# First alibi pass inside the last rope sequence, second pass from its end on, and far ranks by ScalarE

## The chip, the cores and the metric

The kernel runs on one core of one Trainium2 chip. The metric is the device time of one execution in microseconds, the median of several runs. All times of the profile come from one profiled execution.

## What is computed

Four layers over a tensor of 4 sequences of 512 tokens with 128 channels. Each layer normalises its input, computes an attention-like branch `s` and a gate `g` from a mixture of experts, and adds their product:

```python
xn = _layernorm(x); s = attn(xn); g = _silu(ffn(xn)); x = x + s * g
```

The change touches the end of layer 2 (rope attention, eight small experts) and layer 3. In layer 2

```python
att_num = exp(q_rope @ k_rope * scale)
att_den = sum(exp(q @ k * scale), axis=-1)
y = (att_num / att_den) @ v
```

In layer 3, 16 heads of width 8 with a linear bias by distance, and an expert layer with 16 experts that each take the 160 tokens which chose them with the highest probability:

```python
scores = q @ k.T / sqrt(8) - abs(i - j) * 0.5**h
out = softmax(scores) @ v
top1_val, top1_idx = probs.max(-1), probs.argmax(-1)
masked = where(top1_idx == expert, top1_val, -inf)
vals, idx = top_k(masked, 160)        # ceil(1.25 * 2048 / 16)
y[idx] = gelu(x[idx] @ W1 + b1) @ W2 + b2   # tokens not taken keep their input
```

## The kernel before

**Lists of steps.** `flow()` returns one list of steps (what, layer, sequence, number). Each engine's program walks the same list and issues its share of each step, so this list, written by hand, is the order of TensorE, VectorE, ScalarE, GpSimd and the DMA queue of SyncE. Engines are coupled by semaphores only. The last rope sequence stands in `rope_alone()`, layer 3 in `last_layer(tail)`, where `tail` is the end of the last rope sequence ("t" 0 to 3: turn the heads, project, combine, norm and turn).

**Scores.** A unit is two banks of PSUM, 1024 columns: two heads by one block of 128 keys or queries. A quad is four heads. For the alibi layer each sequence has 32 first-pass units ("a", `scores_a`, lines 1200 and 1214), each of which VectorE reduces to negated row maxima (`maxima`, line 2088), and 32 second-pass units ("b", `scores_b`, lines 1253, 1273 and 1277), whose exponential ScalarE takes (`probabilities`, line 1674). Between them stands "mx": the maxima are turned on TensorE (line 1222), split in two, and go through DRAM into rows of the second pass's operand (`maxima` of SyncE). A rope sequence has no maxima: 32 plain units (line 1260), whose exponentials are only summed (line 1657), and 32 rotated ones (line 1264, exponential on line 1674). "pv" multiplies probabilities with values (`values`, line 1295, for the alibi layer, `grain_values`, line 1314, for the others), "bc" turns the sums and divides ("heads").

**Two slots.** The four banks of scores are two slots. They are given to "a" and "b" units in turn, in the order of the list, whatever their kind. A unit waits until the unit before the last has been read.

**Buffers.** Rope and causal probabilities go through a ring of four buffers ("grains") of two units each. The alibi layer has two buffers of four units each. Its operands are three stacks for each parity of the sequence, `stacks3`; those of sequence 0 are filled by DMA after the rope list has ended (`part_out`, line 2372: six DMAs for each of queries and keys; `last_stacks`, line 2376: 24 DMAs; `rows`), the rest after that.

**Order of layer 3.** The rope list ends; then 32 "a" units of sequence 0 stand alone with the rope tail, the expert logits ("lg", line 1116), their softmax ("sm", `route_softmax` and `route_parts`), eight transposes ("tn") and 12 ranks. Then for b = 1, 2, 3: second pass of sequence b - 1 with the 32 "a" units of sequence b spread among it. Sequence 3's second pass comes last.

**Ranks.** 64 steps "rk" (`route_row`, line 1131, and `route_rank`, line 2010). Step n compares 128 tokens (block n // 4) with 512 tokens (sequence n % 4): TensorE writes a row of 512 values, VectorE counts in one pass how many are above the token's own. The 16 steps in which the 512 hold the 128 (near ranks) are cut in two pieces and have a third operation for ties. After 16 ranks "sl" makes slot numbers, with which GpSimd scatters tokens to DRAM. After the last it loads all slots (line 2282); "xt" turns them, "eu" and "ed" are the experts in pairs (gelu on line 1722), "xb" turns them back (line 1728), and GpSimd writes them (line 2284) and gathers them by token (line 2289, 16 gathers), after which "t" 2 of each sequence ends the layer.

## Time and profile before

| | us |
|---|---|
| median of 3 runs (lowest to highest) | 1894.1 (1892.93 to 1896.52) |
| time of the profiled execution | 1889.69 |
| its span, first to last instruction | 1887.6 |
| PE busy | 1542.4 (82%) |
| DVE busy | 1178.3 (62%) |
| ACT busy | 995.9 (53%) |
| POOL busy | 206.5 (11%) |
| mean granted TensorE clock | 0.866 of 2.4 GHz |

PE is TensorE's matmuls, DVE is VectorE, ACT is ScalarE, POOL is GpSimd, SPq SyncE's DMA issues. Matmuls are pipelined, so busy PE time is longer at the lower of TensorE's two clock levels (1.2 GHz, a granted clock of 0.5) and says nothing of how well the array is filled. Times in the trace are microseconds from the start of the span. In a row of a stretch, busy times are sums in us inside it, (x) is the count of instructions, PEclk the mean granted clock. In a row of the timeline, the first number is the start, the second the length; brackets name idle time of that engine just before and what ended it.

### The profile page before, as it was taken

Reading aid. Unit: us, or ns where it says so; the run is one execution under the profiler, and the core shown is the slowest. Engines: PE = TensorE matmul, PEld = TensorE weight load, DVE = VectorE, ACT = ScalarE, POOL = GpSimd, SP = SyncE. Lnnn points to the kernel's source line nnn. Section 1 sums busy time; section 2 is a strip of 40 time slices with the busy share of each in tenths; the row PEclk is TensorE's granted clock in tenths of the full one; section 3 lists DMA queues with packets and bytes.
Section 4 is the critical chain, followed back from the end, with each engine's and each line's share of the span. In section 5 each row is a group of like instructions: output and inputs, shape, how many; then the busy total and the mean of one; then the engine's idle time right before and its main releaser. Section 6 shows DMA issues by size and latency. Waiting matters only on the chain. (4 is left out here: it accounts for less than half of the span.)

```text
span 1887.6 us, 23967 instructions
## 1 busy us (share of the span) xinstructions
PE 1542.4 (82%) x8656; PEld 778.0 (41%) x8656; DVE 1178.3 (62%) x2370; ACT 995.9 (53%) x1642; POOL 206.5 (11%) x152
## 2 busy tenths in 40 slices
PE   5999989988699588977889778897586578878886
PEld 2555556555355244433444334443232322323442
DVE  4789989999765853456534665335425787776522
ACT  4787778866123147633666326654574122333675
POOL 1333342432000000000000000000000000001003
PEclk9999999999899799978998789986666567888999
DMA  4422232353301120203002030001402142122002
GB/s 169 119 75 73 78 81 68 90 143 93 106 19 51 51 60 10 63 22 101 19 1 76 9 101 19 18 1 36 109 19 83 46 164 59 33 65 60 1 2 73
DMA packets 91621, 116.30 MB, mean 62 GB/s; under 512 B 10096, under 2 KB 71536, under 8 KB 91120
## 3 DMA queue, kind: packets, MB, share of 16 engines
q1 hardware_dynamic: 89808, 110.05, 20.8%
q0 software_dynamic: 1696, 4.72, 0.9%
q8 instruction: 69, 1.13, 0.3%
q14 instruction: 48, 0.39, 0.1%
HBM read 83.27 MB, written 31.46 MB: 61 GB/s over the span
## 5 line engine op out<-in xcount | busy, mean ns | idle before, releaser
L1674 ACT ACTIVATE scratch<-ps 128x1024 f32<-128x1024 f32 x272 | 271.3, 1022 | 218.8 <-PE ps L1270 69.7
L2088 DVE TENSOR_REDUCE neg_max<-ps 128x2 f32<-128x1024 f32 (+2 forms) x224 | 234.4, 1068 | 97.8 <-PE ps L1214 97.0
L1657 ACT ACTIVATE ps<-ps 128x512 f32<-128x512 f32 x256 | 150.0, 586 | 84.4 <-PE ps L1260 83.9
L1945 DVE TENSOR_TENSOR_SCAN scratch<-scratch 128x512 f32<-128x512 f32 x128 | 159.5, 1286 | 3.5 <-ACT scratch L1628 3.4
L1853 DVE SCALAR_TENSOR_TENSOR gated<-tanh,ps 128x512 f32<-128x512 f32 x88 | 60.4, 687 | 135.9 <-ACT tanh L1556 135.8
L1314 PE MATMUL ps<-scratch,values 128*32 128x512 f32 (+3 forms) x1024 | 129.7, 598 | 10.4 <-ACT scratch L1674 9.0
L1556 ACT ACTIVATE tanh<-ps 128x512 f32<-128x512 f32 x88 | 52.3, 595 | 160.0 <-PE ps L995 159.7
L1030 PE MATMUL ps<-xnt,weights_even 128*128 128x512 f32 x256 | 125.5, 612 | 7.5 <-ACT gated L1539 6.6
L2268 POOL TENSOR_SCALAR variance_eps<-mean_var 128x4 f32<-128x4 f32 x20 | 5.3, 264 | 978.2 <-DVE mean_var L1773 978.2
L995 PE MATMUL ps<-xnt,weights_odd 128*128 128x512 f32 x176 | 109.6, 708 | 0.0
L2101 DVE COPY head_out<-ps 128x512 f32<-128x512 f32 x48 | 33.0, 688 | 117.0 <-PE ps L1314 76.5
L998 PE MATMUL ps<-xnt,weights_odd 128*128 128x512 f32 x176 | 97.9, 639 | 7.0 <-DVE values L2070 7.0
L1674 ACT ACTIVATE weights_even<-ps 128x1024 f32<-128x1024 f32 x64 | 64.8, 1024 | 72.3 <-PE ps L1277 71.7
L1214 PE MATMUL ps<-scratch 52*128 52x256 bf16 (+7 forms) x704 | 96.3, 343 | 0.0
L1017 PE MATMUL ps<-weights_odd,hidden 128*128 128x128 f32 x640 | 94.5, 292 | 0.0
L1017 PEld LDWEIGHTS ps<-weights_odd,hidden 128*128 128x128 f32 x640 | 81.1, 197 | 29.9 <-issue 28.0
L2307 POOL TENSOR_TENSOR weights_odd<-weights_odd,scratch 128x512 f32<-128x512 f32 x32 | 72.4, 2262 | 170.7 <-DVE scratch L1952 170.3
L1260 PE MATMUL ps<-scratch 48*128 48x512 bf16 x256 | 61.1, 441 | 33.9 <-ACT ps L1657 25.3
L1200 PE MATMUL ps<-consts,scratch 128*128 128x128 bf16 x256 | 42.2, 255 | 55.6 <-DVE neg_max L2088 51.6
L2307 POOL TENSOR_TENSOR scratch<-scratch 128x512 f32<-128x512 f32 x32 | 67.8, 2118 | 131.9 <-DVE scratch L1952 131.7
L1067 PE MATMUL ps<-scratch,consts 128*128 128x512 f32 x128 | 71.4, 641 | 12.5 <-DVE scratch L1952 12.3
L1264 PE MATMUL ps<-scratch 48*128 48x512 bf16 x256 | 57.4, 454 | 29.5 <-DVE neg_max L2088 12.1
(324 smaller groups left out, 2917.6 us busy)
## 6 DMA issues: line engine op xcount, KB each, us to landing
scratch<-state_rows SPq DMA_DIRECT2D x64, 512.0 KB, 4.9
scratch<-parts_scratch SPq DMA_DIRECT2D x288, 96.0 KB, 2.4
parts_scratch<-weights_even SPq DMA_DIRECT2D x168, 128.0 KB, 2.4
weights_odd<-in_l SPq DMA_DIRECT2D x8, 519.5 KB, 6.4
weights_even<-in_l SPq DMA_DIRECT2D x1, 4096.0 KB, 15.9
weights_odd<-in_l SPq DMA_DIRECT2D x1, 4096.0 KB, 12.9
parts_scratch<-gated SPq DMA_DIRECT2D x15, 128.0 KB, 2.4
slots_scratch<-head_out SPq DMA_DIRECT2D x5, 256.0 KB, 5.2
```

Of the source, the lines that this page charges most:

```text
L995: pe.matmul(ps[:, UP, :], W(l, "w1")[:, P * f:P * (f + 1)], tokens(b), start=True, stop=True)\
L998: pe.matmul(ps[:, MI, :], W(l, "w3")[:, P * f:P * (f + 1)], tokens(b), start=True, stop=True)\
L1017: mm = pe.matmul(ps[:, YB, P * j:P * (j + 1)], buf[lo:lo + n, P * j:P * (j + 1)], W(l, "w2")[lo:lo + n, P * src:P * (src + 1)], start=(one ...
L1030: pe.matmul(ps[:, up_bank(0, n), :], W(0, "w1")[:, P * f:P * (f + 1)], tokens(n // NF[0]), start=True, stop=True).then_inc(q[0, "up_ready" ...
L1067: pe.matmul(ps[:, 0, :], eye, hc[n % 3][:, 0, :], start=False, stop=True, skip_group_check=True)\
L1214: mm = pe.matmul(place(col + c0, c1 - c0), lhs, stack_of(l, b, 1 + turn)[p0:p0 + KA[l], s, c0:c1], start=False, stop=True, skip_group_chec ...
L1314: mm = pe.matmul(ps[32 * i:32 * i + 32, PV, q0:q0 + n], vx[l - 1][:, c, VW * h:VW * h + 32], grain(l, b, s)[:, place_, col:col + n], start ...
L1657: ins = act.activation(bank, bank, ACT.Exp, accum_out=dens[:, j, h:h + 1])
L1674: act.activation(dst, src, ACT.Exp).then_inc(q[l, "exp_done"], 1)
L1945: dve.tensor_tensor_scan(hs[:, g, :], da[n % RING][:, g, :], ub[:, g, :], 0.0, ALU.mult, ALU.add)\
L2088: ins = dve.tensor_reduce(dst, ps[:, base:base + 2, col:col + n], AX.X, ALU.max, negate=True)
L2307: pool.tensor_tensor(y1[b % 2], y1[b % 2], hc[n % 3][:, 1, :], ALU.add)\
```

## The change

- The alibi units of the first pass are listed before those of the second, and values go one key block at a time: 16 stages of two units for each sequence in place of 8 of four in two parts. The product is `grain_values` for all layers; `values` goes.
- The ring becomes seven places. Layer 3 uses places 2 and 4 for its first sequence and 2, 4, 5, 6 for the others; the last rope sequence uses three in place of four.
- `stacks3` of sequence 0 moves to space that is free while rope runs; that of sequence 1 takes the space of rope's stacks and two grains.
- `rope_alone` lists the 32 first-pass units of alibi sequence 0 among quads 1 to 3 of the last rope sequence, with the queries and keys of alibi sequences 0 and 1, "mx" of sequence 0 before the last units, and the DMA steps for it.
- `last_layer` begins with the second pass of sequence 0: its first 20 items stand without first-pass units, beside the tail, logits and softmax; the 32 first-pass units of sequence 1 follow. Ranks: 16, 30 and 18 beside b = 1, 2, 3, in place of 12 before b = 1 and 26, 26 and 0. Four expert pairs stand in b = 3 and four in the last pass, in place of five and three.
- Far ranks (48 of 64) go to ScalarE: a Sign with the token's scaled value as bias into SBUF, then a Relu with an accumulator. Near ranks stay on VectorE. Each kind has its own semaphore, and the slot step has two more small VectorE operations.

The core of the diff:

```diff
             sums = [[(h, j, 512 * k, 512) for k, h in enumerate(hp)] for j in range(TB) for hp in pairs]
-            for cp in range(2):
-                for n in range(4):
-                    unit = sums[4 * cp + n]
-                    units_a.append(unit)
-                    units_b.append((len(stages), n, unit))
-                stages.append((g, cp, len(units_b), 2))
+            units_a += sums
+            for j in range(TB):
+                for n in range(2):
+                    units_b.append((len(stages), n, sums[2 * j + n]))
+                stages.append((g, [(j, 0, 0, 512)], len(units_b)))
...
-    out = with_extras(a[0], extras) + [("mx", l, 0, 0)] + ranks(6, 12)
-    cuts = [12, 38, RANKS]
+    out, cuts = [], [0, 16, 46, RANKS]
     for b in range(1, NB):
         main = stream[begin[b - 1]:begin[b]]
-        cover = len(main) - 10
-        main = spread(main[:cover], a[b]) + [("mx", l, b, 0)] + main[cover:]
-        extras = [(18, ("v", l, b, 0))] if b > 1 else [(2, ("v", l, 1, 0))]
+        cover, alone = len(main) - 10, 20 if b == 1 else 0
+        main = main[:alone] + spread(main[alone:cover], a[b]) + [("mx", l, b, 0)] + main[cover:]
+        route = ranks(cuts[b - 1], cuts[b])
+        if b == 1:
+            out.append(tail[0])
+            extras = [(1, tail[1]), (5, tail[2]), (8, ("v", l, 1, 0)), (12, tail[3])]
+            extras += [(14, ("lg", l, 0, 0)), (15, ("sm", l, 0, 0)), (18, ("sm", l, 0, 1))]
+            extras += [(22 + 2 * k, ("tn", l, 0, k)) for k in range(8)]
+            extras += [(40 + 40 * n // len(route), item) for n, item in enumerate(route)]
+        else:
+            extras = [(18, ("v", l, b, 0))]
         if b + 1 < NB:
-            extras += [(34, ("q", l, b + 1, 0)), (40, ("q", l, b + 1, 1))]
...
+            extras += [(44, ("q", l, b + 1, 0)), (50, ("q", l, b + 1, 1))]
+        if b == 2:
             extras += [(3 + 78 * n // len(route), item) for n, item in enumerate(route)]
-        else:
-            extras += [(28 + 3 * n, ("xt", l, 0, n)) for n in range(ST // 4)]
-            for p in range(5):
-                extras += [(44 + 8 * p, ("eu", l, 0, p)), (48 + 8 * p, ("ed", l, 0, p))]
+        if b == 3:
+            extras += [(n, item) for n, item in enumerate(route)]
+            extras += [(40 + 3 * n, ("xt", l, 0, n)) for n in range(ST // 4)]
+            for p in range(4):
+                extras += [(54 + 8 * p, ("eu", l, 0, p)), (58 + 8 * p, ("ed", l, 0, p))]
...
-    extras += [(18 + n, ("xb", l, 0, n)) for n in range(ST // 4)]
+    for p in range(4, PAIRS):
+        extras += [(2 + 5 * (p - 4), ("eu", l, 0, p)), (4 + 5 * (p - 4), ("ed", l, 0, p))]
+    extras += [(23 + n, ("xb", l, 0, n)) for n in range(ST // 4)]
...
+    a = [("a", 3, 0, n) for n in range(2 * TB * QUADS)]
+    groups = [(rope_sums(c, g),) + rope_group(c, g) for g in range(QUADS)]
+    sums, group, bc = groups[0]
+    out += weave(sums, tail2[0:2] + head[5:7])
+    out += weave(group, tail2[2:3] + [("mb0", 2, c, 0), ("mb1", 2, c, 0), ("set", 3, 0, 0), ("q", 3, 0, 0)]) + [("q", 3, 0, 1)]
+    sums, group, last = groups[1]
+    out += [("ld", 2, c, 2)] + later(weave(later(sums, bc), tail2[3:4] + d[0:2]), u[0:2], 4)
+    out += weave(group, a[0:4], d[2:4]) + u[2:4]
+    sums, group, bc = groups[2]
+    out += [("ld", 2, c, 3)] + weave(later(sums, last), a[4:11], d[4:6])
+    out += weave(group, a[11:18], d[6:8])
+    sums, group, last = groups[3]
+    out += weave(later(sums, bc), a[18:25], [("v", 3, 0, 0), ("q", 3, 1, 0)])
+    out += weave(group[:6], a[25:32], [("q", 3, 1, 1)]) + [("mx", 3, 0, 0), ("ld", 3, 1, 0)] + group[6:]
+    return out + [last], [("t", 2, c, k) for k in range(4)]
...
-        pt3 = [scratch[:, 12288:16384].rearrange("p (i c) -> p i c", i=4), wa[:, PT_AT:PT_AT + 4096].rearrange("p (i c) -> p i c", i=4)]
+        ring = [v.rearrange("p (i c) -> p i c", i=4) for v in
+                [scratch[:, n:n + 2048] for n in (8192, 10240, 12288, 14336, 4096)] + [wa[:, n:n + 2048] for n in (PT_AT, PT_AT + 2048)]]
+                    for n in ns] for ns in ((0, 1, 7), (3, 4, 5))]
...
+            if l == 3:
+                return (2, 4, 5, 6) if b else (2, 4)
+            return (0, 1, 2) if l == 2 and b == NB - 1 else (0, 1, 2, 3)
...
+                def rank_far(n):
+
+                    i, c = n // TB, n % TB
+                    above = c > i // TB
+                    act.wait_ge(q[3, "row_ready"], n + 1)
+                    done, count = ranked(n)
+                    if count > 2:
+                        act.wait_ge(done, count - 2)
+                    sign = r_sign[count % 2]
+                    own.link(act.activation(sign, ps[:, route_bank(n), :], ACT.Sign, scale=-RANK_SCALE, bias=r_v[:, 1, i:i + 1]))
+                    counter = c if above else 6 + c
+                    act.activation(sign, sign, ACT.Relu, scale=-1.0 if above else 1.0,
+                                   accum_out=r_acc[:, i, counter:counter + 1]).then_inc(done, 1)
...
+                elif what == "q" and l == 3 and b == 1:
+                    part_out(l, b, n)
+                elif what == "ld" and l == 3:
+                    sp.wait_ge(q[2, "pv_done"], NS[2] * NB)
+                    rows(l, odd=True)
+                    last_stacks(b)
+                    load_columns(3, at["l3"]["w1"][0], wide["l3"], s_w[3])
...
+                elif what == "mx" and (l == 1 or b == 0):
+                    maxima(l, b)
+                elif what == "q" and l == 3 and b == 0:
+                    part_out(l, b, n)
                     if n == 1:
-                        rows(3)
...
+                        sp.wait_ge(q[fourth[0], "pv_done"], fourth[1])
+                        rows(l)
+                        last_stacks(b)
```

## Rows read from the trace of the kernel before

**Rows 1.** Busy time by stretch; columns as in the first line, us.

```profile
core 0: us, PE busy (x) PEld busy (x) DVE busy (x) ACT busy (x) POOL busy (x), PEclk, DMA share, GB/s
1330.00:1391.00 61.00, 45.67 (x208) 20.25 (x208) 19.04 (x76) 43.00 (x91) 2.53 (x4) 0.61 0.25 67
1391.00:1442.00 51.00, 38.83 (x188) 13.47 (x185) 13.11 (x37) 37.53 (x84) 0.00 (x0) 0.70 0.28 80
1442.00:1530.50 88.50, 55.63 (x278) 26.78 (x276) 71.99 (x173) 8.25 (x14) 2.53 (x4) 0.54 0.22 62
1530.50:1627.80 97.30, 79.72 (x519) 26.34 (x518) 71.50 (x146) 32.91 (x33) 7.95 (x8) 0.77 0.25 84
1627.80:1724.10 96.30, 78.07 (x552) 26.62 (x550) 71.88 (x151) 34.52 (x35) 6.66 (x7) 0.84 0.16 46
1724.10:1815.90 91.80, 77.33 (x622) 37.24 (x620) 49.72 (x61) 54.56 (x68) 2.36 (x3) 0.93 0.09 24
1815.90:1872.00 56.10, 49.24 (x419) 22.47 (x418) 8.65 (x20) 46.66 (x57) 12.76 (x13) 1.00 0.14 37
1872.00:1887.60 15.60, 2.41 (x16) 1.74 (x16) 9.32 (x15) 2.78 (x5) 3.77 (x4) 0.73 0.32 88
```

**Rows 2.** Waits of TensorE, 1442 to 1530.5: us in total, times, longest.

```profile
PE ps L1200 <- DVE neg_max L2088: 23.4, 12, 8.6
```

**Rows 3.** Timeline of TensorE: logits, turning of maxima, first unit of the second pass.

```profile
1472.73 7.01 PE L1116 MATMUL ps<-weights_odd,xnt 128*128 128x16 f32 x32
...
1523.28 1.01 PE L1222 MATMUL ps<-consts,neg_max 128*16 128x128 f32 x4 [0.62 <-DVE neg_max L2088]
...
1530.56 0.42 PE L1253 MATMUL ps<-consts,scratch 128*128 128x128 bf16 x2
```

**Rows 4.** Timeline of TensorE: a rope unit, values, a first-pass unit (two rows).

```profile
1402.93 0.61 PE L1264 MATMUL ps<-scratch 48*128 48x512 bf16 x2 [1.04 <-ACT ps L1657]
...
1406.49 1.93 PE L1314 MATMUL ps<-scratch,values 128*32 128x512 f32 x8
...
1448.92 0.39 PE L1200 MATMUL ps<-consts,scratch 128*128 128x128 bf16 x2
1449.24 0.61 PE L1214 MATMUL ps<-scratch 52*128 52x512 bf16 x2
```

**Rows 5.** Groups of VectorE instructions, 1627.8 to 1724.1: busy us, mean ns | idle before.

```profile
L2088 DVE TENSOR_REDUCE neg_max<-ps 128x2 f32<-128x1024 f32 x32 | 39.1, 1223 | 14.4 <-PE ps L1214 14.3
L2010 DVE TENSOR_SCALAR_CACHE_REDUCE weights_even<-ps,weights_even 128x512 bf16<-128x512 f32 (+3 forms) x32 | 20.2, 644 | 4.2 <-PE ps L1131 4.0
...
L2010 DVE DVE_READ_ACCUMULATOR weights_even<-ps,weights_even 128x1 f32 x32 | 2.6, 83 | 0.0
```

**Rows 6.** Groups of ScalarE instructions, 1391 to 1442.

```profile
L1657 ACT ACTIVATE ps<-ps 128x512 f32<-128x512 f32 x32 | 18.6, 583 | 3.1 <-PE ps L1260 3.1
L1674 ACT ACTIVATE scratch<-ps 128x1024 f32<-128x1024 f32 x16 | 15.5, 1020 | 6.9 <-PE ps L1264 6.9
L1657 ACT ACTIVATION_READ_ACCUMULATOR ps<-ps 128x1 f32 x32 | 6.0, 187 | 0.0
...
L1641 ACT ACTIVATE queries_keys<-ps,small_l 128x512 f32<-128x512 f32 x1 | 0.7, 688 | 1.1 <-PE ps L1165 1.1
```

**Rows 7.** Timeline of TensorE: turning of the normed rows of rope sequence 2.

```profile
1352.54 1.09 PE L982 MATMUL ps<-consts,branch 128*128 128x128 f32 x4 [5.00 <-DVE branch L1786]
```

**Rows 8.** Timeline of SyncE's DMA queue: stack loads of alibi sequence 0.

```profile
1429.07 11.04 SPq L2376 DMA_DIRECT2D scratch<-parts_scratch  x22
```

**Rows 9.** Groups of ScalarE instructions, 1724.1 to 1872: table loads and gelus.

```profile
L1722 ACT ACT_TABLE_LOAD x8 | 10.3, 1283 | 0.1
...
L1722 ACT ACTIVATE hidden<-ps,weights_odd 128x160 f32<-128x160 f32 x32 | 10.0, 395 | 6.3 <-PE ps L1142 6.2
```

**Rows 10.** Timeline of GpSimd: write of the slots, last of 16 gathers.

```profile
1846.30 1.33 POOL L2284 DMA_DIRECT2D slots_scratch<-weights_even  x1 [117.63 <-ACT weights_even L1728]
...
1877.28 0.94 POOL L2289 DMA_INDIRECT weights_even<-slots_scratch,logits  x1 [0.30 <-issue]
```

169 lines of the change are left out of this document (58 added, 111 removed).

## Prediction

> **What bounds the kernel now.** I read the page for its shares first, then the table of busy time by stretch, cut at the places where the step list changes its work [rows 1], then the waits of TensorE in the stretch that the change empties, then single instructions for prices. Columns of [rows 1] to compare: the length, PE, DVE and ACT busy, and PEclk.
>
> Call the stretches R1 (1330 to 1391) and R2 (1391 to 1442), the last rope sequence; A (1442 to 1530.5), the first alibi pass alone; B0, B1, B2 (to 1627.8, 1724.1, 1815.9), a second pass beside the next first pass; B3 (to 1872), the last second pass; and the tail. In R2 ScalarE works 37.5 of 51.0 us and VectorE 13.1. In A it is the other way round: VectorE 72.0 of 88.5, ScalarE 8.3, TensorE 55.6 at a granted clock of 0.54, so nearly all of it at 1.2 GHz. There TensorE waits 23.4 us for maxima [rows 2]. In B0 and B1 VectorE (71.5 and 71.9) and TensorE (79.7 and 78.1) hold each other up: two score slots are handed out in turn, so a first-pass unit waits for the reduction before it, and that queues behind ranks. In B3 TensorE has 49.2 of 56.1 and ScalarE 46.7. VectorE's surplus in A is thus what the whole end pays for, and the change spreads it.
>
> **The change part by part.** Terms are in the span of the profiled execution, 1887.6 us; its own time is 1889.7, and the median of the three runs 1894.1, 4.4 above it.
>
> *A goes.* Its 88.5 us end [rows 1] with the way of the maxima through DRAM: turned at 1523.28, first second-pass unit at 1530.56, 7.3 us [rows 3]. The new list turns them before the last three rope units; a rope unit with its share of values takes 1.6 us or more (51.0 / 32 in R2), and with three values blocks and the last quad's heads these cover about 8 us. Cover gone, at most 7.3. Term: -88.5.
>
> *R1 and R2 take 32 first-pass units.* Such a unit is 0.39 + 0.61 us of TensorE at the low level [rows 4] (about two thirds of that at 2.4 GHz, an estimate from the L1200 and L1214 lines of other stretches) and one reduction of 1.22 us [rows 5], on a VectorE that has 13.1 us to do in R2. But the slots: rope units now go two to a slot pair with a maxima unit between nearly all of them, so neither kind is double buffered any more. One period of a pair is scores 0.8, reduction 1.22, two handovers of 0.1 to 0.2: 2.3 us, longer than the rope side, which is 0.6 of scores and 2 x 0.583 + 0.19 of exponentials [rows 4, 6]. 28 pairs lie in R2: 64 us. On top come 8 values blocks of 1.93 at the low level [rows 4], taken at 1.4 because part of them fits into the pair's gaps: 11. Projections of queries, keys and values, heads and expert downs: 9. So R2 goes from 51 to 84: +33. In R1, 4 units at 1.2: +5. R1 also gains and loses a wait of the same size: the turning of the normed rows, for which TensorE stood 5.0 us [rows 7], moves later, while the first maxima unit now waits for operands. That DMA queue I followed: six pieces each of queries and keys, 3.8 us each, seven row loads, then 24 stack loads of 0.5 us (22 took 11.04 [rows 8]) with the next rope stack queued behind them. The rope stack has over 20 us to spare; the first quad's stack lands about 5 us after TensorE could use it, and all later rope units would queue behind that unit on TensorE, and ScalarE behind them. I set the two against each other. Term: +38, bounds +22 (pairs at 2.0, values half hidden) and +60 (pairs at 3.0, as in B1, 96.3 / 32).
>
> *B0 changes its inside.* First part: 14 second-pass units without maxima units, at 1.5 us each (B3 gives (56.1 - 3 expert pairs of about 3.8) / 32 = 1.4): 21. Beside them the tail of the rope layer, turns and values (5 us of TensorE), the logits, 7.0 us of TensorE [rows 3], and a softmax behind which ScalarE's exponentials queue because its exp is in the same stream: about 5. Together 38. Its operands (30 loads and the expert weights, released by the last rope values) have these 38 us to land. Second part: 32 maxima units beside 12 second-pass units. VectorE: 32 x 1.22 = 39, parts of the next queries and keys 4.5, heads 3, near ranks 4: 51. TensorE at 2.4 GHz also comes to about 50. Two engines both full and coupled by the slots: 60. The last ten items as now: 9.5. B0 becomes 108: +11, bounds 0 and +22. Only two buffers hold probabilities for this sequence, two units each; the values block that frees one stands ahead of the unit that needs it in TensorE's order, so I price that at 0; so too the two small sums (0.17 each) that each of the four blocks of slot numbers gains.
>
> *Ranks change engine.* A rank costs VectorE 0.64 + 0.08 [rows 5]. 48 of the 64 are far ones. On ScalarE each is two activations: the nearest rows are 0.688 for one with a pointer bias out of PSUM, 0.583 for one with an accumulator and 0.19 for its read [rows 6], and the second waits for the first, so 1.5 us (1.2 if they overlap, 1.8 if each link costs a handover). In B1, 22 of 30 ranks are far: VectorE loses 16 us, ScalarE goes from 34.5 to about 68 of 96.3. Before B1's TensorE was idle for 18.2 us; I take half of that back: -9 (0 to -18). The Trainium skill, ScalarE: Activation LUTs, "Rules for kernel authors", speaks against this edit: it puts max, relu and the like on VectorE, up to three times faster per element. The trace agrees in the ratio (1.5 against 0.72 here); it disagrees in what it is worth, since the row of B1 shows ScalarE idle for two thirds of the time. By the rule alone the edit would cost 48 x 0.8 = 37 us; that is not the sum's value, but near the slower rival below.
>
> In B2, 18 ranks now stand one behind each of the first 18 items. 14 far ones are 21 us of ScalarE beside 8 exponentials, 29 us where these items took 18/85 of 91.8 = 19: +10, less one expert pair, which leaves for B3 (two table loads of 1.283 and four gelus of 0.395 [rows 9], 4.1): +5, bounds -4 and +12. The slots' way through DRAM (17.5 us by the same trace) begins some 25 us later and is asked for 12 items later; 23 items lie between, enough.
>
> *B3 and the tail.* One pair more, 4 us, and the turning back of the slots moves from item 18 to 23: GpSimd's chain of write and gathers, which runs from 1846.3 to the last issue at 1877.3 plus landing [rows 10] and cannot be shortened, starts about 7 us later after B3's begin. It ended just before the last sums now, so most of this shows: +6, bounds +3 and +9.
>
> Sum: -88.5 + 38 + 11 - 9 + 5 + 6 = -37.5. Span 1850.1, profiled time 1852.2, median 1856.6.
>
> **The rivals.**
> *Clock.* With pairs in R2 TensorE is asked for more, and it may be granted 2.4 GHz where it had 0.61 and 0.70 [rows 1]. B2, at 0.93, and B3, at 1.00, where TensorE waits least, show the level held. Then pairs take 2.0, values 1.07, B0 and B1 give 8 each more: about 22 us better, 1834.
> *Slot pairs at the pace of B1.* If coupling costs as much as in B1, 3.0 a pair, R2 gains another 20 and B0 8: 1884. For it: VectorE's stream has expert sums and parts between the reductions. Against: B1's pace holds a rank in each pair.
> *Far ranks on the path (slower).* Place: ScalarE's stream in B0 to B2, where exponentials queue behind a rank and TensorE behind these through the slots. Price: 48 x 1.5 = 72 us if all of it shows, in place of B1's -9. The other terms sum to -28.5, so it decides from 0.6 us a rank. Against: ScalarE is idle 60 us of B1; for: in B2 they come one to every item. With two thirds exposed: -28.5 + 48 = +20, 1914.
> *Table loads (slower).* If Sign were in another table set than the exponential, each far rank would bring two loads of 1.283 [rows 9]: 48 x 2.57 = 123 us of ScalarE, of which at most 60 hides: 1920 or more. No operation of the trace is a Sign. The Trainium skill, same page, "Table sets: the hidden batching unit", says cheap functions stand in every set and names relu but not sign; it prices a switch at 2.66 us, by which this would be 255 us, and which no row here shows (1.283 and 0.1 idle).
> *The move does nothing.* Maxima units in R2 wait for their stacks until rope has ended: then A's reductions come back, +25, 1882. The queue count above speaks against it.
>
> **How the numbers follow.** Forecast (within 15 us of 1856.6) 0.60; clock 0.15; slot pace or late stacks 0.13; far ranks 0.09; table loads 0.03. The range goes from 1830, the clock's case with a margin, to 1888, which holds the slot rival, and leaves out the two slower ones and the extremes. Within 0.2% (3.8 us, about what a measurement of this kernel can tell from no change) lie the mildest far-rank cases and the worst of the slot rival: 0.04. Slower 0.10, faster 0.86.
>
> **What would show it.** Right: maxima units from about 1380 on, the last rope values near 1480, no stretch in which ScalarE does under a third; PE busy over 80% there; far ranks of 1.2 to 1.8 us with no table load in front; the gathers as the last thing waited for. Wrong: a pair above 2.8 us in R2; TensorE waiting for exponentials in B1 (then ranks are on the path); a wait of over 10 us for a stack; clock still under 0.7 in R2, which by itself makes 84 into 95.

## The result, and the profile after

The changed kernel took 1881.5 us (median of 14 runs, 1869.9 to 1888.1) against 1894.0 for the kernel before beside it (14 runs): a ratio of 0.9921, 95% interval 0.9903 to 0.9938, a gain of about 15 us by the ratio and 12.4 by the medians. The sum had said 37.5. Two more sets with the same kernel gave 0.9946 and 0.9897 (controls below), so the change is worth 0.5 to 1.0%, 10 to 20 us. Its profiled execution took 1880.9 us, with a span of 1879.1 (1887.6 before).

Busy time by stretch after, cut where the steps of [rows 1] now lie: R1, R2 with the first pass inside, B0, B1, B2, B3 and the tail; columns as there.

```profile
core 0: us, PE busy (x) PEld busy (x) DVE busy (x) ACT busy (x) POOL busy (x), PEclk, DMA share, GB/s
1330.30:1391.30 61.00, 45.22 (x205) 20.49 (x206) 25.58 (x84) 40.94 (x89) 2.53 (x4) 0.61 0.52 121
1391.30:1483.40 92.10, 68.52 (x377) 24.45 (x376) 50.76 (x74) 43.46 (x88) 0.00 (x0) 0.67 0.11 29
1483.40:1595.50 112.10, 87.36 (x586) 35.57 (x584) 74.23 (x186) 55.14 (x82) 3.12 (x5) 0.77 0.33 100
1595.50:1699.90 104.40, 84.96 (x555) 28.83 (x556) 59.15 (x106) 64.11 (x105) 7.42 (x8) 0.77 0.16 44
1699.90:1802.70 102.80, 84.12 (x622) 38.48 (x622) 57.00 (x105) 67.41 (x102) 9.02 (x9) 0.88 0.09 25
1802.70:1861.00 58.30, 51.66 (x432) 24.54 (x432) 8.68 (x21) 50.01 (x63) 9.95 (x10) 1.00 0.12 32
1861.00:1879.10 18.10, 4.12 (x20) 2.98 (x16) 9.99 (x16) 2.78 (x5) 6.67 (x7) 0.53 0.32 87
```

Against [rows 1], length less PE busy gives TensorE's idle time:

| stretch | length before, after | forecast, measured | TensorE idle before, after | PE busy before, after |
|---|---|---|---|---|
| A | 88.5, 0 | -88.5, -88.5 | 32.9, 0 | 55.6, 0 |
| R1 + R2 | 112.0, 153.1 | +38, +41.1 | 27.5, 39.4 | 84.5, 113.7 |
| B0 | 97.3, 112.1 | +11, +14.8 | 17.6, 24.7 | 79.7, 87.4 |
| B1 | 96.3, 104.4 | **-9, +8.1** | 18.2, 19.4 | 78.1, 85.0 |
| B2 | 91.8, 102.8 | +5, +11.0 | 14.5, 18.7 | 77.3, 84.1 |
| B3 + tail | 71.7, 76.4 | +6, +4.7 | 20.1, 20.6 | 51.7, 55.8 |

The two right-hand columns are the ones to read. The 55.6 us that TensorE was busy in A came back to within a microsecond in the other stretches (busy 426.9 in all before, 426.0 after), so nearly all that this execution gained (8.5 us of span) is idle time: 32.9 in A against 25 that grew elsewhere. A's work had run at the low level (PEclk 0.54) and the forecast allowed it to be cheaper beside other work; it wasn't, because the level fell in the passes. The share of time at 1.2 GHz is (1 - PEclk) / 0.5: over the whole of [rows 1] it is 257 us before and 250 after. A's 81 us at the low level mostly came back: 30 more in R1 and R2, 7 in B0, 17 in B1, 12 in B2 and 9 in the tail. In B1 this accounts for the length: of its +8.1 us, 6.9 are TensorE busy and 1.2 idle, and 17 us more at the low level, busy for about four fifths, make work of 7 us take 14 (an estimate from these rows).

The next rows are for the steps that came as forecast. Timeline of TensorE: the first moved unit, four pairs of R2, the turning of the maxima, the first second-pass unit.

```profile
1379.23 0.37 PE L1219 MATMUL ps<-consts,scratch 128*128 128x128 bf16 x2 [0.77 <-DMA scratch<-parts_scratch]
...
1456.42 0.39 PE L1219 MATMUL ps<-consts,scratch 128*128 128x128 bf16 x2 [0.90 <-DVE neg_max L2096]
1458.68 0.39 PE L1219 MATMUL ps<-consts,scratch 128*128 128x128 bf16 x2 [0.90 <-DVE neg_max L2096]
1460.94 0.39 PE L1219 MATMUL ps<-consts,scratch 128*128 128x128 bf16 x2 [0.90 <-DVE neg_max L2096]
1463.20 0.39 PE L1219 MATMUL ps<-consts,scratch 128*128 128x128 bf16 x2 [0.90 <-DVE neg_max L2096]
...
1473.63 1.01 PE L1241 MATMUL ps<-consts,neg_max 128*16 128x128 f32 x4 [1.41 <-DVE neg_max L2096]
...
1483.43 0.28 PE L1272 MATMUL ps<-consts,scratch 128*128 128x128 bf16 x2
```

Starts 2.26 us apart are the pair period (2.3 forecast): each time the wait for the reduction ends last. The stacks were late by 0.8 us only, and the first second-pass unit did not wait for its maxima.

Groups of ScalarE and VectorE in B1 after (busy us, mean ns | idle before):

```profile
L1664 ACT ACTIVATE scratch<-ps 128x1024 f32<-128x1024 f32 x17 | 17.0, 1013 | 9.6 <-PE ps L1296 9.6
L1675 ACT ACTIVATE weights_even<-ps,weights_even 128x512 bf16<-128x512 f32 x23 | 15.7, 683 | 17.0 <-PE ps L1150 14.9 <-issue 2.0
L1677 ACT ACTIVATE weights_even<-weights_even 128x512 bf16<-128x512 bf16 x23 | 14.5, 629 | 0.7
L1677 ACT ACTIVATION_READ_ACCUMULATOR weights_even<-weights_even 128x1 f32 x23 | 4.3, 187 | 0.0
```

```profile
L2096 DVE TENSOR_REDUCE neg_max<-ps 128x2 f32<-128x1024 f32 x32 | 39.1, 1223 | 25.7 <-PE ps L1233 25.7
```

A far rank is 683 + 629 + 187 ns, the 1.5 us of the sum, with no table load. But VectorE's relief, 12.7 us busy in B1 (71.9 to 59.2), turned up as its own waiting for score units: 25.7 us where [rows 5] has 14.3. Waits of TensorE there:

```profile
PE ps L1219 <- DVE neg_max L2096: 11.3, 10, 3.1
PE ps L1272 <- DVE neg_max L2096: 2.9, 2, 1.5
PE ps L1272 <- ACT scratch L1664: 2.2, 6, 0.7
PE ps L1313 <- DVE heads_out L2116: 1.6, 2, 0.8
```

14.2 us for maxima, where the same view of before has 15.6:

```profile
PE ps L1200 <- DVE neg_max L2088: 9.2, 10, 1.7
PE ps L1253 <- DVE neg_max L2088: 6.4, 5, 2.4
```

### The profile page after: what moved, and what is told of

The parts are those of the page before. It is cut to its first block and busy times, and to the rows that moved or that the text cites. A ratio compares the mean times of both kernels' runs of the same rounds, so it can differ in the third digit from the quotient of the medians.

```text
span 1879.1 us, 24050 instructions
## 1 busy us (share of the span) xinstructions
PE 1542.9 (82%) x8656; PEld 778.9 (41%) x8656; DVE 1148.0 (61%) x2283; ACT 1059.4 (56%) x1786; POOL 207.9 (11%) x152
## 5 line engine op out<-in xcount | busy, mean ns | idle before, releaser
L1664 ACT ACTIVATE scratch<-ps 128x1024 f32<-128x1024 f32 x288 | 287.2, 1021 | 203.4 <-PE ps L1283 75.2
L1313 PE MATMUL ps<-scratch,values 128*32 128x512 f32 (+3 forms) x1344 | 180.1, 624 | 16.2 <-ACT scratch L1664 10.1
L1233 PE MATMUL ps<-scratch 52*128 52x256 bf16 (+7 forms) x704 | 94.8, 338 | 0.0
L1049 PEld LDWEIGHTS ps<-xnt,weights_even 128*128 128x128 f32 x256 | 50.6, 199 | 74.3 <-issue 65.2
L1283 PE MATMUL ps<-scratch 48*128 48x512 bf16 x256 | 57.1, 448 | 29.6 <-DVE neg_max L2096 15.1
L1959 DVE TENSOR_TENSOR scratch<-scratch 128x512 f32<-128x512 f32 x128 | 80.7, 669 | 0.0
## 6 DMA issues: line engine op xcount, KB each, us to landing
weights_even<-in_l SPq DMA_DIRECT2D x1, 4096.0 KB, 15.6
```

The costliest lines, as they stand in the source:

```text
L1049: pe.matmul(ps[:, up_bank(0, n), :], W(0, "w1")[:, P * f:P * (f + 1)], tokens(n // NF[0]), start=True, stop=True).then_inc(q[0, "up_ready" ...
L1233: mm = pe.matmul(place(col + c0, c1 - c0), lhs, stack_of(l, b, 1 + turn)[p0:p0 + KA[l], s, c0:c1], start=False, stop=True, skip_group_chec ...
L1313: mm = pe.matmul(ps[32 * i:32 * i + 32, PV, q0:q0 + n], (vx[b % 2] if l == 3 else vx[l - 1])[:, c, VW * h:VW * h + 32], grain(l, b, s)[:, ...
L1664: act.activation(dst, src, ACT.Exp).then_inc(q[l, "exp_done"], 1)
L1959: tt(hc[n % 3][:, g, :], hs[:, g, :], bc_rows[n % RING][:, 1, :], ALU.mult).then_inc(q[0, "hc_ready"], 1)
```

## The experiments

A ratio is always to the kernel before, in runs shared by the set; one per cent is 18.9 us. Where profiles are compared, I cut at the turned maxima of sequences 0 to 3, a mark that all kernels have: "pass 1, 2, 3" lie between them, "last" after them. Edits are shown in short.

### First set: who reads the ranks

**All ranks on VectorE, in the new order.**

```diff
-        mine = own_block(n)
+        mine = by_vector(n)        # always true
+        ts(r_junk[:, 0:T], row, mine, 0.0, ALU.is_gt if above else ALU.is_lt, ALU.add, accum_out=...)
```

> The changed kernel with every one of the 64 ranks counted by VectorE again, the far ones with one comparison of the row each; nothing else is different. Theory P (the far ranks' Sign and Relu on ScalarE hold up exponentials and so TensorE in the last alibi passes): 8 to 15 us below the changed kernel, near 1870. Theory Q (TensorE, the maxima and the two score slots set the pace of the alibi passes, and who reads the ranks is of no account): within 4 us of the changed kernel, 1878 to 1886, with VectorE's waiting on score units in the second pass falling back from 25.7 us to about 14. Theory C (TensorE's granted clock in that pass, 0.77 for 0.84, took the time): same time, unless the clock rises with it.

Measured: 1890.5, ratio 0.9972 (0.9952 to 0.9991), 5 to 14 us slower than the changed kernel's three ratios, not faster. Theory P falls, and "of no account" (Q) with it. Pass 2 took 107.5 us (clock 0.75), where the three profiles of the changed kernel have 101.3, 100.6 and 97.4 (0.80, 0.84, 0.89), but TensorE's idle time in it was 19.9 us against 19.2 to 21.1: what ScalarE's ranks gained there lay in the level, not in waiting.

**Far ranks by ScalarE in the old order.**

```diff
-                        route_rank(n)
+                        if own_block(n):
+                            route_rank(n)       # the far ones: rank_far(n) on ScalarE
```

> The kernel before with only the ranks changed: the 48 far ones by ScalarE (Sign, then Relu with a sum), VectorE keeps its 16 own-block ones; the order of all work and its buffers stay. Theory P: 8 us or more above the kernel before, since 48 ranks of 1.5 us stand before exponentials. Theory Q: within 4 us of the kernel before. My prediction's own term (VectorE relieved of 0.64 us a far rank gives TensorE half of its idle time in the second pass back) asks for 5 to 10 us below the kernel before.

Measured: 1892.6, ratio 0.9977 (0.9953 to 1.0001), about 4 us below before and not clear of no change. This is the sum's term for B1 tested by itself, and pass 2 shows none of it: 97.2 us for 96.6 before, TensorE idle for 18.1 us for 18.0. VectorE, busy for 58.1 us in place of 72.3, waited 18 us longer for score units instead. The wait in pass 2 of before, then here:

```profile
DVE neg_max L2088 <- PE ps L1214: 14.3, 13, 3.9
```

```profile
DVE neg_max L2117 <- PE ps L1225: 32.3, 22, 7.9
```

**Without the far ranks' reading**, then also **without most of their rows.**

```diff
-                    own.link(act.activation(sign, ps[:, route_bank(n), :], ACT.Sign, ...))
-                    act.activation(sign, sign, ACT.Relu, ..., accum_out=...).then_inc(done, 1)
+                    act.sem_inc(done, 1)
```

> The changed kernel with the Sign and Relu of the 48 far ranks left out (ScalarE only signals in their place), so that the slots of the tokens are not the reference's; TensorE still makes the rows. Theory P: 12 to 20 us below the changed kernel. Theory Q: less than 5 us below. Theory C: less than 5 us below, with the second pass's clock still at 0.77.

```diff
+                w_ = T if own_block(n) else 32
-                pe.matmul(ps[:, route_bank(n), :], r_hott[...], r_partst[:, T * c:T * (c + 1)],
+                pe.matmul(ps[:, route_bank(n), 0:w_], r_hott[...], r_partst[:, T * c:T * c + w_],
```

> As the kernel without the far ranks' Sign and Relu, and TensorE's row for each far rank is 32 columns wide for 512, so that 48 matmuls of about 0.4 us shrink too; the slots are not the reference's. Theory Q: a further 10 to 20 us below the kernel that left out only the Sign and Relu, since TensorE's own time is what counts. Theory P: less than 5 us further. Theory C: no gain, or a loss, if fewer columns let the granted clock fall.

Measured: 0.9883 (0.9840 to 0.9926) and 0.9841 (0.9798 to 0.9885). From the kernel with all on VectorE, leaving out the 48 readings gains 0.89%, 17 us or 0.35 each; on ScalarE they cost the difference to 0.9921, 7 us or 0.15 each. The rows cost 8 us, 0.17 each. With four runs of each of these kernels, only the 17 us are clear of their interval; the 7 and the 8 are not (each is plus or minus some 9 to 12 us). Together they suggest 0.3 to 0.5 us for a far rank beside two passes, reading and row; no theory's figure (12 to 20 us for P, under 5 for Q and C, then 10 to 20 more for Q) was met.

### Second set: the late items and the clock

**The changed kernel again.**

> The changed kernel once more, nothing edited, as the control of this set and to see which parts of its trace come again. Theory C (in the second and third passes of the last layer, between the turned maxima of sequences 1 and 3, TensorE works at about 0.46 score units per us where it has the low clock and 0.75 where it has the high one, and the changed kernel had the low one for 60 of 207 us there against 27 of 188 in the kernel before) wants a low share well above that of the kernel before again. If it falls to that of the kernel before with the same length, the clock is no cause. Time: 1878 to 1884.

Measured: 1880.3, ratio 0.9946 (0.9927 to 0.9965), span 1873.2. At the low level between the turned maxima of sequences 1 and 3, by (1 - PEclk) / 0.5: 68 us (before 49), length 206.2 (before 187.9). By the same formula the first profile of the changed kernel has 76 and that of the fourth set 57, so the level comes again above that of before, by 8 to 27 us. (The 60 and 27 of the expectation were counted otherwise.) Passes 2 and 3:

```profile
1579.86:1680.42 100.56, 80.07 (x555) 27.54 (x556) 60.47 (x115) 64.73 (x108) 8.46 (x8) 0.84 0.16 46
1680.42:1786.05 105.63, 86.96 (x608) 37.16 (x609) 56.35 (x103) 65.60 (x100) 9.03 (x9) 0.83 0.09 25
```

**Denominators one item earlier.**

```diff
-                    waiting.append((u + lag + 2, ("bc", g)))
+                    waiting.append((u + lag + 1, ("bc", g)))
```

> The changed kernel with the denominators of each four heads one item earlier in the order of the last layer, so that the values block of the next four heads no longer stands directly behind them on TensorE (where it waited 0.8 us for VectorE to read the block before). Theory M (the new order of the late items costs the alibi passes their time): 5 to 12 us below the changed kernel. Theory C: within 4 us of it.

Measured: 1874.8, 0.9932 (0.9908 to 0.9955), no difference from the control that its interval can tell; repeated in the fourth set.

**One, and two, idle matmuls ahead of each first-pass unit of sequences 2 and 3.**

```diff
+                    if l == 3 and b > 1:
+                        for h, j, col, n in ua[u][:1]:      # [:2] for two
+                            pe.matmul(place(col, T), <the unit's own keys>, <its queries>, start=True, ...)
```

> The changed kernel with one matmul of 512 columns more, of no use, ahead of each of the 64 first-pass units of sequences 2 and 3 (0.21 us at the high clock, 0.43 at the low one, overwritten by the unit itself). Theory C with the falls of the clock coming from TensorE's idle stretches: less time at the low clock between the turned maxima of sequences 1 and 3 (under 40 us for 60), and a time from 8 below to 3 above the changed kernel, though 14 to 27 us of TensorE's work were added. If the falls come for another reason, or TensorE's own work simply sets the pace: 8 to 20 us above it. Theory M says nothing of it.

> As the kernel with one such matmul, with two of them ahead of each of the 64 units (27 us of work at the high clock, 55 at the low one). At the high clock TensorE was idle for about 0.33 us in each unit, so 0.42 no longer hides. Theory C: no stretch of low clock left in these passes and 0 to 10 us above the changed kernel; falls for another reason: 20 us or more above it.

Measured: 1.0045 (1.0026 to 1.0063) with one, 0.9997 (0.9974 to 1.0020) with two. Twice the useless work costs half the time: 19 us over the control with one, 10 with two. The clock is the reason that the runs show; passes 2 and 3 with one, and with two:

```profile
1585.11:1699.22 114.11, 99.79 (x588) 30.50 (x589) 60.48 (x115) 65.21 (x106) 8.00 (x8) 0.75 0.14 41
1699.22:1813.15 113.93, 98.66 (x639) 39.98 (x640) 56.72 (x103) 65.64 (x100) 9.00 (x9) 0.82 0.08 23
```

```profile
1578.85:1685.36 106.51, 90.01 (x620) 29.34 (x621) 60.49 (x115) 65.16 (x108) 8.14 (x8) 0.85 0.15 43
1685.36:1792.47 107.11, 89.90 (x671) 38.13 (x672) 56.34 (x103) 65.44 (x100) 9.02 (x9) 0.92 0.08 24
```

At the low level: 98 us with one, 49 with two. PE busy with the 64 idle matmuls is 18.5 us above that with 128. The two profiles exaggerate a little (that with two is of an execution 6 us below its median), but over all executions of each, whole spans, the kernel with one has 495 us at the low level and the kernel with two 467, against 482 for the control. Theory C's expectation for one (less low time, a time near the control) was wrong: one matmul per unit lowered the level, two kept it better. The 19 us are what it gave for the case that TensorE's own work sets the pace; with two, its 0 to 10 us came true, but not the level without a fall. TensorE's idle time in the two passes does not order them either: 39.2 us in the control, 29.6 with one, 33.7 with two.

### Third set: where the clock is low, and what was only placed

**A split of the far ranks.** From rank 46 on with VectorE, denominators early.

```diff
+            return own_block(n) or (n >= 46)
```

> The changed kernel with the denominators one item earlier, and the 14 far ranks of the third pass (from rank 46 on, one behind each item while ScalarE is at 67 of 103 us) back on VectorE with one comparison each; the 34 before them stay on ScalarE. If the price of ranks in the third pass is ScalarE's, 4 to 8 us below the kernel with the earlier denominators alone (ratio to before near 0.990); if it is TensorE's rows or the clock, within 3 us of it (near 0.993).

Measured: 0.9888 (0.9865 to 0.9910), pass 3 in 102.2 us. Near the changed kernel's best set, and the figure that was expected if ScalarE's price counts in pass 3; but without a control in this set, the 6 us to the first 0.9921 are not told apart from nothing.

**Idle matmuls ahead of the last rope sequence's units, and ahead of the second-pass units that stand alone.**

```diff
+                    if l == 2 and b == NB - 1:      # two, with the unit's own operands, overwritten by it
...
+                    if l == 3 and b < NB - 1 and (u >= 24 or u < (14 if b == 0 else 6)):
```

> The changed kernel with two matmuls of 512 columns of no use ahead of each of the 64 units of the last rope sequence (27 us of TensorE's work at the high clock, 55 at the low one), where the clock is 0.61 to 0.69. Theory C, with falls that come from TensorE's idle stretches: the clock rises above 0.85 there and the stretch from 1330 to the first turned maxima is no longer than before to 15 us shorter. If the falls have another reason: the clock stays under 0.75 and the time is 20 to 40 us above the changed kernel.

> The changed kernel with two matmuls of 512 columns of no use ahead of those second-pass units that have no first-pass unit beside them (14 at the start of the first pass, and the last 8 and first 6 of each), where TensorE is idle for a third of the time and the clock has fallen by the end of each pass. Theory C: the low stretches around the turned maxima go and the time is 0 to 10 us below the changed kernel. Falls for another reason: 5 to 20 us above.

Measured: 0.9951 (0.9935 to 0.9966) and 0.9921 (0.9906 to 0.9937). The rope stretch to the first turned maxima:

```profile
1330.00:1488.19 158.19, 122.55 (x661) 45.34 (x662) 76.17 (x159) 82.29 (x173) 2.53 (x4) 0.68 0.28 68
```

In the three profiles of the changed kernel this stretch takes 140.3 to 143.6 us, PE busy 101.7 to 105.5, clock 0.64 to 0.67. The fillers thus added 17 to 21 us of busy time and raised the clock to 0.68 only, not above 0.85. Over the whole stretch they hardly took idle time away (35.6 us for 38.1 to 40.5), so the stretch as a whole says little of whether idle time keeps the level low. One part of it does; here with the fillers, and then in the changed kernel (fourth set):

```profile
1420.00:1450.00 30.00, 27.68 (x154) 9.79 (x154) 15.07 (x23) 12.08 (x20) 0.00 (x0) 0.59 0.00 1
```

```profile
1420.00:1450.00 30.00, 22.21 (x143) 8.44 (x141) 19.52 (x32) 14.82 (x34) 0.00 (x0) 0.78 0.00 1
```

Busy for 92% of these 30 us, TensorE has the lower clock, so idle time alone does not explain the low level in rope. The profile is also of its slowest execution, 1900.7 us where the median is 1889.4, so its 158.2 us overstate the cost; the kernel as a whole was 1 to 10 us above the changed one's three ratios, not 20 to 40. At the edges, pass 3 rose to 0.87 where all three profiles have 0.83, and pass 2's 0.87 lies within their 0.80 to 0.89. The lengths, 101.4 and 105.7, did not change: in pass 3 the added work ate what the level gave.

**The kernel before with the new placement.** Far ranks on ScalarE and cuts, slots and pairs as in the change; the pass stays where it was.

```diff
-    out = with_extras(a[0], extras) + [("mx", l, 0, 0)] + ranks(6, 12)
-    cuts = [12, 38, RANKS]
+    out = with_extras(a[0], extras) + [("mx", l, 0, 0)]
+    cuts = [0, 16, 46, RANKS]
```

> The kernel before with the far ranks on ScalarE and, in the last layer, the ranks, slots and expert pairs placed as in the changed kernel (none beside the first alibi pass, 16, 30 and 18 beside the three passes, slots read from item 40, four pairs beside the third pass); the first alibi pass stays after the rope sequence. My sum priced this placement at about nothing: first alibi pass some 6 us shorter, the second and third passes +5, the last +6. Theory R (each rank beside two passes costs 0.5 us or more of TensorE's order, and those of the first pass cost nothing since TensorE waits there): 8 to 20 us above the kernel before, with the third pass at 100 or more for 91.3. Theory C alone: within 5 us of the kernel before.

Measured: 1.0013 (0.9995 to 1.0031). That is 2.5 us above the kernel before, within the 5 of theory C; theory R, with 8 to 20 and a third pass of 100 or more, falls. Against the same ranks at their old place (0.9977, another set) the new placement costs 0.36%, 6.8 us, plus or minus 6. In the sum the placement is the +5 of B2 and the +6 of B3, less the ranks that left A with its 88.5 (some 6 by the expectation): about the right size. Passes 1 to 3 and last:

```profile
1517.93:1612.83 94.90, 66.19 (x444) 21.12 (x444) 52.09 (x75) 42.04 (x61) 0.00 (x0) 0.76 0.31 101
1612.83:1709.96 97.13, 80.67 (x554) 26.82 (x555) 60.34 (x115) 63.62 (x103) 7.96 (x8) 0.82 0.17 47
1709.96:1805.37 95.41, 79.50 (x607) 33.46 (x608) 55.90 (x103) 65.46 (x100) 9.04 (x9) 0.91 0.10 27
1805.37:1898.00 92.63, 68.17 (x532) 33.39 (x532) 22.05 (x44) 61.97 (x79) 17.10 (x17) 0.89 0.14 38
```

### Fourth set: the move by itself, and a better place for the ranks

**The pass put back.** Blocks of two units, order of late items, early operands and placement stay; the rope tail, logits and softmax go back beside the pass.

```diff
-    a = [("a", 3, 0, n) for n in range(2 * TB * QUADS)]      # in rope_alone
+    a = []
-    out, cuts = [], [0, 16, 46, RANKS]                        # in last_layer
+    out, cuts = with_extras(a[0], extras) + [("mx", l, 0, 0), ("ld", l, 1, 0)], [0, 16, 46, RANKS]
```

> The changed kernel with its first alibi pass put back behind the last rope sequence (with rope tail, logits and softmax among it, as before); its operands' early loads, its order of late items, its blocks of two units, its ranks and slots stay. Against the kernel before with ranks placed (1.0013 of before, passes between the turned maxima 94.9, 97.1 and 95.4 us) it shows what the new blocks and order of late items cost: theory M wants the second and third passes at 100 or more (1.005 to 1.012 of before); if they come back to 97 and 95, the move itself, or the clock with it, lengthens them (1.000 to 1.003).

> The changed kernel once more, nothing edited, as the control of this set: 0.992 to 0.995 of the kernel before, passes of 107 to 111, 100 to 102 and 105 to 106 us.

Measured: 1905.0, 1.0045 (1.0028 to 1.0063), with pass 2 back at 97 and pass 3 not, and for the changed kernel beside it 1872.2, 0.9897 (0.9870 to 0.9924). The move alone is thus worth 1.48%, 28 us plus or minus some 6, against 19.5 for the whole change in this set. The result lies between what the two theories asked for. The pass put back, and then the control, passes 1 to 3 and last:

```profile
1509.30:1613.59 104.29, 77.62 (x443) 22.96 (x444) 52.08 (x75) 42.42 (x61) 0.00 (x0) 0.61 0.36 109
1613.59:1710.43 96.84, 77.01 (x554) 26.95 (x555) 60.22 (x115) 63.33 (x103) 8.18 (x8) 0.87 0.17 48
1710.43:1815.98 105.55, 86.82 (x608) 37.09 (x608) 56.38 (x103) 65.60 (x100) 9.00 (x9) 0.83 0.09 25
1815.98:1903.60 87.62, 64.20 (x532) 31.14 (x532) 22.02 (x44) 61.65 (x79) 17.23 (x17) 0.94 0.15 41
```

```profile
1470.31:1577.66 107.35, 82.37 (x556) 31.77 (x557) 72.94 (x177) 50.44 (x73) 2.53 (x4) 0.79 0.35 108
1577.66:1675.07 97.41, 76.30 (x556) 26.89 (x557) 60.49 (x115) 64.43 (x108) 7.94 (x8) 0.89 0.17 47
1675.07:1780.54 105.47, 86.70 (x607) 37.01 (x608) 56.38 (x103) 65.68 (x100) 9.01 (x9) 0.83 0.09 25
1780.54:1868.80 88.26, 66.03 (x532) 32.56 (x532) 21.93 (x44) 61.64 (x79) 16.71 (x17) 0.90 0.15 40
```

Pass 3 is the clean comparison: 607 or 608 matmuls in each, 95.4 us with the old blocks (clock 0.91), 105.5 with the new ones (0.83), wherever the first pass stands, and 105.6 at 0.83 in the two other profiles of the changed kernel. 7.3 of the 10.1 us are PE busy, as many instructions at the lower level; 2.8 are idle time. So the new blocks and order, not the move, lengthen pass 3. Which of the two does it these runs don't separate; the place of the denominators alone moves pass 3 by 2 to 6 us (next).

**Denominators one item earlier, again.**

> The changed kernel with the denominators one item earlier, beside a control of its own on the same chip. Theory M: 4 to 8 us below the control, by the 0.8 us that a values block waited for the denominators' reader sixteen times. Theory C: within 2 us, with the difference between profiles of one pass (94.9 for 101.3) a matter of when the clock fell.

Measured: 0.9899 (0.9874 to 0.9924), level with the control. Its pass 3 took 99.4 us (clock 0.88) for 105.5, but its pass 1 took 116.0 (0.72) for 107.3 (0.79); in the second set it was 103.2 and 112.9. The order of late items sets where the level falls, and what pass 3 wins pass 1 lost. Theory M holds for a pass and not for the kernel.

**Ranks early.** Far ranks from 46 on with VectorE, denominators early, and:

```diff
-    out, cuts = [], [0, 16, 46, RANKS]
+    out, cuts = [], [0, 24, 52, RANKS]
-            extras += [(40 + 3 * n, ("xt", l, 0, n)) for n in range(ST // 4)]
-            for p in range(4):
+            extras += [(34 + 3 * n, ("xt", l, 0, n)) for n in range(ST // 4)]
+            for p in range(5):         # "eu" from 47, "ed" from 51, "xb" from 19 in the last pass
```

> The kernel with the earlier denominators and the far ranks from 46 on with VectorE, and with its 64 ranks cut at 24 and 52 for 16 and 46, so that the slots begin 6 items earlier in the third pass; the slots are read from item 34, five expert pairs stand in the third pass, and the slots go back from item 19 of the last one. If GpSimd's chain at the end is what the last pass waits for, 3 to 6 us below the control; if the passes only take over what the tail gives up, within 2 us of the kernel that split the ranks (0.988 to 0.992 of before).

> The kernel with early ranks (cut at 24 and 52, slots 6 items earlier, far ranks from 46 on with VectorE), but with the denominators back at the place of the changed kernel, directly ahead of the next values block. If the order of late items matters only in the third pass and is paid back in the first, it is within 3 us of the kernel with the earlier denominators beside it (0.984 to 0.987 of before); if the earlier denominators carry the gain of that kernel, it is 4 us or more above it, near 0.990.

> The kernel with early ranks and earlier denominators once more, to see whether its 0.984 of the kernel before comes again: 0.982 to 0.987, passes of 110 to 118, 97 to 99 and about 95 us and 85 us after the last turned maxima.

Measured: 1864.8, 0.9842 (0.9818 to 0.9865); with the denominators back in place 0.9882 (0.9856 to 0.9909); the first again, beside the latter, 1864.2, 0.9872 (0.9847 to 0.9897). Early ranks beat the control by 0.55%, 10 us plus or minus 7, and have the lowest times of all complete kernels here; the place of the denominators again makes no difference that can be told (0.9872 and 0.9882). Two places gave the time: after the last turned maxima the three profiles with early ranks take 82.2 to 85.1 us for 87.2 to 88.3, and pass 3 takes 94.8 to 98.0 for 105.5, while pass 1 loses a few (112.0 to 117.9 for 107.3 to 110.7). Behind the last turned maxima it is GpSimd's chain, which writes the slots 42 to 45 us after them for 48 in the changed kernel. Pass 3 has 12 ranks for 18, with the far ones on VectorE, and one expert pair more; the far ranks on VectorE and the earlier denominators had brought it to 102.2 in the third set, and no run separates the rest. GpSimd's last gather, in the changed kernel and in the first and the repeated one with early ranks:

```profile
1870.04 1.02 POOL L2297 DMA_INDIRECT weights_even<-slots_scratch,logits  x1 [0.30 <-issue]
```

```profile
1860.30 1.14 POOL L2309 DMA_INDIRECT weights_even<-slots_scratch,logits  x1 [0.30 <-issue]
```

```profile
1849.65 1.15 POOL L2309 DMA_INDIRECT weights_even<-slots_scratch,logits  x1 [0.30 <-issue]
```

The spans are 1879.1, 1869.5 and 1858.9: each ends 9.1 to 9.3 us after this issue (before, 10.3 [rows 10]; 8.0 to 11.8 over all kernels here). From the write of the slots to the last gather it is 31.0 to 31.8 us in every one of them, so the write of the slots sets the end to within some 4 us.

## Why the prediction was wrong, point by point

**Right.** A went; R1 and R2 took 41.1 us more for +38, with pairs at 2.26 us, the maxima's way through DRAM covered and the stacks in time; B0 came to +14.8 for +11, B3 and tail to +4.7 for +6. The price of a far rank on ScalarE and the missing table load were right. That R1 and R2 came near is in part luck: R1 kept its 61.0 us and R2 took all 41.1. Together the move (A, R and B0: -39.5 forecast) gave -28 by the ratios, -34.8 by the spans of the two profiles (1903.6 and 1868.8).

**The term that failed** is the -9 of B1, "I take half of that back", where "that" is TensorE's 18.2 us of idle time, and with it the +5 for B2. They measured +8.1 and +11.0, together 23 of the 29 us that the profiled span fell short, and the idle time of B1 went to 19.4. Three errors are in it:

1. *Relief that no one was waiting for.* B1's TensorE waited 15.6 us for maxima before and 14.2 after. VectorE, busy for 12.7 us less, waited 11.4 more for units instead. The same edit in the old order left pass 2 at 97.2 us for 96.6, with 18.1 us of idle time for 18.0. It gave 4 us of the kernel there, at the edge of what can be told, and about 10 in the new order (0.9972 to 0.9921, from different sets), but by the level in pass 2 and not by TensorE's waiting.
2. *The level in B1 and B2 was taken as it was.* The sum has no term for a fall from 0.84 to 0.77 and from 0.93 to 0.88. With 17 and 12 us more at the low level, TensorE's busy time rose by 6.9 and 6.8 us. The four ranks more in B1 are part of it (26 to 30; some 1 to 2 us by the price above); the placement as a whole, which the sum had about right, cost 6.8 us.
3. *The blocks of two units had no price.* The sum looked at the values block that frees a buffer and says "I price that at 0". With the same placement and the pass put back, they and the early operands cost 6 us, plus or minus 5 (1.0013 to 1.0045): 8.6 us less before the first turned maxima, 9.4 and 10.1 more in passes 1 and 3, 5.0 less in the last. I looked for a wait on a buffer; the cost is mostly TensorE's level (pass 1 at 0.61 for 0.76, pass 3 at 0.83 for 0.91).

In ratios: far ranks -4.4 us, placement +6.8, blocks and early operands +6.1, the move -28.0. They add up to -19.5, the value of the fourth set, by construction, since each step is a difference of two ratios. Placement and blocks go across sets, and the sets of the changed kernel differ by 9 us, so no term is known better than to some 4 to 6 us.

Two slips of the working changed little. By the list of steps, 23 of the 30 ranks of B1 are far and 13 of the 18 of B2, not 22 and 14. And the clock rival's parts (28 pairs at 0.3 less, 8 values blocks at 0.33 less, 8 each for B0 and B1) come to 27 us, not 22.

**The clock.** The rival with this name expected TensorE's higher level in R and 8 us each from B0 and B1. R stayed at 0.61 and 0.67, and the passes fell. How much a fall costs can be estimated from one kernel's executions. Between 1330 and the end, the three profiles of the changed kernel were at the low level for 250, 219 and 213 us with spans of 1879.1, 1873.2 and 1868.8: 0.28 us for each microsecond between the first and the last, but 0.19 and 0.73 between neighbours. All 31 executions of this kernel, span against (1 - clock) / 0.5 of it, lie about a line of 0.3 (correlation 0.87), the executions of the kernel before about one of 0.4 (0.85). The kernel before had 107 us at the low level after its first turned maxima, the changed kernel 147, 125 and 120: at 0.3 to 0.4, some 4 to 16 us of the 34 to 41 by which this part grew. The growth stands in pass 1 (95.1 us before, 107.3 to 110.7 after), pass 3 (91.3, then 105.5) and behind the last turned maxima (81.4, then 87 to 88). The Trainium skill, TensorE: Matmul & The Clock Gate, "HAM oscillation — how this bites in real kernels", takes half of the time at the low level as lost. By that page it would be 7 to 20 us, an estimate; by the executions here it is less, probably because part of the slower work only filled idle time, which no run here shows.

**The other rivals.** *Far ranks on the path* fell: taking their reading away gained 7 us (16 at most), not 48, and putting them back on VectorE lost time. *Slot pairs at the pace of B1*: R2 ran at 2.26, B1 at 3.3 (104.4 / 32). *Table loads* and *the move does nothing* did not happen. The time, 1881.5, lies where the slot rival's 1884 was, for another reason; that it lies inside 1830 to 1888 it owes to the breadth of the range and not to the sum.

**What a check would have told.** TensorE's busy time is its work at its level. A sum of -37.5 asks for 37.5 us less idle time or for a higher level. A had 32.9 us of idle time; R2's pairs bring back some (11.9 measured in R1 and R2; each pair holds 0.9 us of waiting), B0's coupling some (7.1). With these measured values about 14 us are left to gain without a change of level, and the 9 of B1 would have had to come out of its 18.2. The working summed lengths and never held them against this account.

**What stays open.** Why the last rope sequence stays near the low level even where TensorE is busy for 92% of the time, why two idle matmuls in a unit kept the level better than one, and so how to order the passes so that it stays high. Whether the blocks of two cost anything where the level doesn't fall was not tried.

## What to carry to other kernels

When work moves beside other work, write down for each stretch the idle time and the level of the engine that ends up full, before and after; with the same work, what it gains cannot be more than the idle time that goes plus what the level gives. The idle time was visible in the first table. Relieving an engine pays only where the waits on it end last, and moving small steps into a full stretch has a price per step though their engine has room. And look at what the very last chain hangs on: the kernel whose ranks and slots come earlier was 10 us faster here, about half of it after the last turned maxima, where GpSimd's fixed 31 us of gathers set the end.

## What the runs showed of the hardware

- Twice the idle work can cost less time: two passes took 206.2 us as they are, 228.0 with 64 idle matmuls of 512 columns and 213.6 with 128, with 68, 98 and 49 us at the low level.
- The level differs between executions of one kernel: pass 2 ran at 0.80, 0.84 and 0.89 (101.3, 100.6 and 97.4 us). Over 31 executions the mean clock of the changed kernel goes with its span, from 1870 to 1888 us, at about 0.3 us for each microsecond at the low level.
- A Sign from PSUM (683 ns), a Relu with a sum in SBUF (629) and its read (187) stand between exponentials without a table load; the accumulator's read costs 187 ns on ScalarE and 83 on VectorE [rows 5].
